# Where the experts' results are stored from: SyncE's queue or ScalarE's

## The reference, cut to what matters

```
buf = jnp.zeros((E, C, D), dtype=x.dtype).at[chosen_e, pos_c].add(x_flat * kept[:, None].astype(x.dtype))
h = jax.nn.gelu(jnp.einsum('ecd,edf->ecf', buf, w1) + b1[:, None, :], approximate=False)
eo = jnp.einsum('ecf,efd->ecd', h, w2) + b2[:, None, :]
y = eo[chosen_e, pos_c] * (chosen_p * kept.astype(x.dtype))[:, None]
```

## Time and profile before

| | us |
|---|---|
| Median of three runs (3335.19 to 3336.39) | 3335.85 |
| The profiled execution | 3335.44 |
| Its span, first to last instruction | 3333.7 |

### The profile page before, as it was taken

The page is one execution under the profiler, slowest core; times in us unless marked ns, Lnnn a source line. Parts: engine busy times, 40 slices in busy tenths (PEclk is TensorE's granted clock), DMA queues, the critical chain, the costliest instruction groups (busy, mean ns, idle before and its releaser), DMA issues. The chain is left out here.

```text
span 3333.7 us, 98254 instructions
## 1 busy us (share of the span) xinstructions
PE 3019.8 (91%) x27585; PEld 2232.3 (67%) x27741; DVE 2417.5 (73%) x8136; ACT 2248.4 (67%) x8822; POOL 1391.3 (42%) x2572
## 2 busy tenths in 40 slices
PE   7999998999999999999999996777996999977777
PEld 4555555788888888888888874555664666654444
DVE  6888887677777777777777773114665899978886
ACT  6888887666666666666666663224774999975554
POOL 5777775122222222222222210004663777757775
PEclk9999999999999999999999998998997999989999
DMA  5000000100000000000000001221000000000000
GB/s 150 0 0 0 0 0 11 70 5 6 5 4 4 5 4 5 5 5 5 5 5 4 12 3 46 68 77 30 17 17 6 7 6 7 6 4 7 13 19 13
DMA packets 80374, 54.49 MB, mean 16 GB/s; under 512 B 24801, under 2 KB 74413, under 8 KB 80160
## 3 DMA queue, kind: packets, MB, share of 16 engines
q1 hardware_dynamic: 76192, 45.26, 4.8%
q0 software_dynamic: 4096, 8.16, 0.8%
HBM read 32.66 MB, written 20.97 MB: 16 GB/s over the span
## 5 line engine op out<-in xcount | busy, mean ns | idle before, releaser
L1100 DVE COPY b_prT<-b_tr 128x512 f32<-128x512 f32 x512 | 352.0, 687 | 237.8 <-PE b_tr L991 233.4
L1359 ACT ACTIVATE b_pr<-b_sc,b_low 128x205 f32<-128x205 f32 x1024 | 431.1, 431 | 33.9 <-DVE b_low L1076 33.9
L473 ACT ACTIVATE a_pr<-a_sc,a_low 128x128 f32<-128x128 f32 x1024 | 360.8, 387 | 11.7 <-DVE a_low L376 6.9
L1091 DVE TENSOR_SCALAR b_pn<-b_pr,b_rec 128x205 f32<-128x205 f32 x1024 | 298.5, 334 | 55.0 <-DVE b_rec L1085 0.3
L1417 POOL TENSOR_TENSOR b_ln_var<-b_ln_mean_var,all_eps 128x1 f32<-128x1 f32 x64 | 12.1, 189 | 757.8 <-DVE b_ln_mean_var L152 757.8
L991 PE MATMUL b_tr<-all_ident,b_pn 128*128 128x128 f32 x2048 | 323.0, 280 | 5.3 <-DVE b_prT L1100 3.1
L2149 ACT ACTIVATE f_pr<-f_sc,f_low 128x77 f32<-128x77 f32 x1024 | 316.0, 333 | 13.8 <-DVE f_low L2057 13.7
L512 POOL TENSOR_TENSOR a_pn<-a_pr,a_rec 128x512 f32<-128x512 f32 x256 | 261.2, 1042 | 123.1 <-DVE a_rec L384 106.8
L991 PEld LDWEIGHTS b_tr<-all_ident,b_pn 128*128 128x128 f32 x2048 | 227.0, 141 | 87.0 <-issue 79.2
L1076 DVE TENSOR_REDUCE b_low<-b_sc 128x4 f32<-128x820 f32 x256 | 256.2, 1001 | 9.3 <-PE b_sc L979 9.3
L979 PE MATMUL b_sc<-b_kT,b_q 64*128 64x205 f32 x2048 | 247.2, 359 | 0.0
(11 more groups left out here) (307 smaller groups left out, 8170.5 us busy)
## 6 DMA issues: line engine op xcount, KB each, us to landing
scratch_x<-b_zeros SPq DMA_DIRECT2D x12, 512.0 KB, 5.2
b_vm<-scratch_x SPq DMA_DIRECT2D x24, 256.0 KB, 3.0
scratch_y<-b_vt SPq DMA_DIRECT2D x24, 256.0 KB, 2.4
all_X<-in_x SPq DMA_DIRECT2D x8, 512.0 KB, 6.9
e_w<-in_e_w SPq DMA_DIRECT2D x16, 256.0 KB, 3.0
out_x<-all_X SPq DMA_DIRECT2D x8, 512.0 KB
w_mask<-in_mask SPq DMA_DIRECT2D x1, 2464.0 KB, 10.3
b_cT<-in_ctxT SPq DMA_DIRECT2D x32, 77.0 KB, 2.0
```

The costliest lines, as they stand in the source:

```text
L473: op = act.activation(pr[:, g, u], sc[:, g, 128 * u:128 * u + 128], ACT.Exp, bias=low[:, g, u:u + 1], scale=-1.0, accum_out=sums[:, g, u:u ...
L1091: op = dve.tensor_scalar(pn[:, j % 2, g, 0:KN], pr[:, j % 2, g, 0:KN], rec[:, j % 2, g:g + 1], None, ALU.mult)
L1100: dve.tensor_copy(prT[:, j % 2, i].rearrange("p h t q -> p (h t q)"), tr[:]).then_inc(prT_made, 1)
L1359: op = act.activation(pr[:, j % 2, g, 0:KN], sc[:, j % 2, h, KN * i:KN * i + KN], ACT.Exp, bias=low[:, j % 2, g:g + 1], scale=-1.0, accum_ ...
```

## The change

The store of a group's results leaves SP's stream and goes to ScalarE's. It stands there behind the four Gelu activations of group n and stores group n-2, ahead of what ScalarE does for the FP4 weights in that step. Its wait for the addition, the buffers and the semaphore that it signals are the same. The last two stores follow the last pair on ScalarE. SP keeps the loads of rows and weights and, at the end, the wait for all stores.

```diff
@@ sync(sp), body @@
                     sp.dma_start(xr[:, k % 2], x_rows[n]).then_inc(x_loaded[k % 2], 16)
-                    if not (isinstance(j, int) and j == 0 and k < 2):
-                        store(n - 2, k % 2)
-
-        def store(n, ring):
-            sp.wait_ge(y_done, n + 1)
-            sp.dma_start(y_rows[n], yr[:, ring]).then_inc(stored[ring], 16)
 
         over_pairs(sp, body)
-        store(N * E // 2 - 2, 0)
-        store(N * E // 2 - 1, 1)
         for s in stored:
             sp.wait_ge(s, 16 * (E // 2) * G)
@@ scalar(act) @@
+
+        def store(n, ring):
+            act.wait_ge(y_done, n + 1)
+            act.dma_start(y_rows[n], yr[:, ring]).then_inc(stored[ring], 16)
 
         def body(j):
...
                     act.activation(hT[k % 2][:, f], ph[:, f // 2, f % 2], ACT.Gelu, bias=b1[:, r, f:f + 1])\
                         .then_inc(h_done, 1)
+                if not (isinstance(j, int) and j == 0 and k < 2):
+                    store(n - 2, k % 2)
                 if isinstance(j, int) and j == 0 and 0 <= k - FIRST - 2 < 3:
                     copy_weight(k - FIRST - 2)
                 if isinstance(j, int) and j == 0 and 0 <= k - FIRST < 3:
                     fp4_magic(act, fp4, consts, k - FIRST, (k - FIRST) % 2)
 
         over_pairs(act, body)
+        store(N * E // 2 - 2, 0)
+        store(N * E // 2 - 1, 1)
```

## The result

| | Median, us | Range | Runs |
|---|---|---|---|
| Before | 3335.52 | 3335.06 to 3336.39 | 4 |
| After | 3281.57 | 3280.56 to 3282.26 | 4 |

The ratio after to before is 0.9838, 95% interval 0.9821 to 0.9855. The profiled execution after took 3280.56 us, with a span of 3278.8.

The account below looks back on a forecast made before the run. TensorE bounds the experts but waits for loads queued on SP behind stores awaiting fresh additions. 39.1 + 10.1 + 2 - 2.55 = 48.7 us, taken as 49, gave 3287 us; range 3283 to 3293.

Parts of the forecast that it names:

- step 3: Pipeline overlap in the experts: each of 19 removed waits hides another 0.06 to 0.16 us; 2 us gained.
- step 5: Weight copies behind the stores on ScalarE make TensorE's transposes of groups 4, 5 and 6 wait: 2.55 us added.
- Step 1: TensorE's 19 waits for gathered token rows in the experts, after the first, all go: 39.1 us gained.
- Step 2: Slow clock in transposes and down matmuls behind the long load waits goes: 10.1 us gained.
- The second count: Check by start times of TensorE's groups up to transpose 23, with steps of 7.55 us: 49.1 us gained.
- Step 4: A store issue on ScalarE behind the Gelus costs 0.4 us, hidden in 21 of 24 groups.
- the clock was given back: Answers the rival that stretches of the experts stay at 1.2 GHz: 10 us less gain, 3297 us; 6%.
- ScalarE did not become the bound: Answers the rival that stores hold ScalarE and delay the next Gelus: 3349 us at 7 us per store; 2%.
- Only the issue time is saved: Rival: something else holds the loads back; 0.4 us in each of 22 steps, 9 us gained, 3327 us; 3%.

Follow-up runs that it names:

- e2: Changed kernel with only the stores ahead of a new expert's weights on ScalarE, the others back on SP: 3299.3 us (0.9883 of before).
- e3: Changed kernel with the stores ahead of a new expert's weights back on SP, the others on ScalarE: 3328.3 us (0.9972 of before).
- e4: Changed kernel with each store split into four DMAs of 64 KB, issued in a row by ScalarE: 3287.3 us (0.9849 of before).
- e5: Changed kernel with the three FP4 weight copies moved ahead of the Gelus of their group: 3278.7 us (0.9822 of before).
- e1: Kernel before with all stores kept on SP, each one slot later, behind the next load: 3282.7 us (0.9834 of before).
- e6: e1 with the three FP4 weight copies moved ahead of the Gelus of their group: 3278.9 us (0.9819 of before).
- e7: e3 with one more SP wait: an expert's second load is issued only when its first has landed: 3325.2 us (0.9957 of before).
- cb2: Kernel before, no edit, profiled a third time, on the same chip as its second profile: 3336.5 us.

## Why the prediction was wrong

The mechanism was right; the sizes of two terms were not. The sum of 48.7 us was 3.4 short of what the stretch gave, 52.1: the pipeline overlap (step 3) was taken at 2 us and measured 4.2, and the added waits (step 5) at 2.55 us and measured 1.4. The other 2 us up to the medians' 54.0 come with a profile of before whose stretch was short, and the range had no room for either.

- **Step 1, the load waits:** all 19 went. The slack at a new expert was smaller than worked out: the 11 us left out the addition's own time. For group 12 the addition ends at 2114.04, the first weight DMA goes out at 2114.28 and the load at 2116.45, and the transposes start at 2123.96, so 9.7 and 7.5 us. The loads took longer, 3.5 us in the median and 5.5 at most, which stayed hidden. Right in what it gives, and worth 39.1 in the profile used, 40.3 in the other two.
- **Step 2, the slow clock:** right in kind; e2 and e3 separate it from the short waits. Its size is not a constant: 10.1 us in the first profile, 12.2 and 11.6 in the two others (89.8 and 15.8 + 0.45 taken off). With step 1 that makes the stretch 3 us longer than in the profile from which I subtracted; by the mean of the three profiles it falls by 54.1 us, as the medians do. The total of the first profile did not give this away, since its time behind the experts was 2.4 us long: 52.1 + 2.4 + 0.4 ahead of the stretch are the 54.9 us between the two profiled executions.
- **Step 3, the pipeline overlap:** the term that was mis-sized in the sum itself. I took 2 us for 19 waits. A wait costs its row and 0.22 us: before, the step from group 16 to 17 took 2199.44 - 2190.85 = 8.59 us with a wait of 0.92, and the same step without takes 7.45, a difference of 1.14. The first 0.16 is the modelled end of up; the other 0.06 is in the transposes, 0.66 behind a wait and 0.60 without. 19 times 0.22 is 4.2. My bounds, 1.1 to 3.0, left out the second part. The lower one was a misreading too: the 3.54 us are those of the up of 3.70 (2041.11 to 2044.65), which also gives 0.16, so the rows had 3.0 to offer where I took the middle. The second count, 3.0 us short, had a fault of the same kind in another place: its step of 7.55 came from the one unwaited step in the trace, and that began with an up of 3.70 us behind a wait for DVE, 0.1 longer than the others. 17 steps make 1.8 us of the 3.0; step 5 makes the rest.
- **Step 4, the issue on ScalarE:** 0.38 us, as priced, and hidden.
- **Step 5, the three places without cover:** wrong by the 0.4 us each. I had the issue after the last Gelu; it runs beside it, and only what is longer than the Gelu would show (e4). The new wait at group 6 came, 1.25 us instead of 1.75. With the overlap, group 6 gives back 9.22 - 7.45 - 0.33 = 1.4 us (0.33 for the three weight transposes, by e5's steps of 7.78 against 7.45), where I took 2.55 for all three. The upper bound of 1.07 us for an issue was not the dearest in the trace either: the scatter's on L1451 take up to 1.23 us; it did not matter.

With the measured sizes the sum is 39.1 + 10.1 + 4.2 - 1.4 = 52.0, and the stretch fell by 52.1.

The rivals: the clock was given back in full. ScalarE did not become the bound. "Only the issue time is saved" is refuted twice, since e1 saves no issue on SP and gains the same, and e6, with the issues on SP, is as fast as e5. The sentence of the Trainium skill (DMA: Bandwidth & Descriptors, Issuing engines are not separate DMA queues) is thereby borne out for what it speaks of: another issuing engine gave nothing here, 3282.7 against 3283.1 us. The gain here was another one: a wait that stood in a queue ahead of a load that did not need it.

## What to carry to other kernels

When an engine waits for a load, look at what its queue waited for ahead of the issue; a store that waits for a fresh result may stand behind the next loads instead of on another engine, and here it gained the same. Price a removed wait by the difference between a step with it and one without, not by its row, and add the slow clock behind the long ones. Where such clock is part of the sum, one profile is one draw: take two or three, or widen the range by what it could have been.

## What the runs showed of the hardware

- A DMA issue in ScalarE's queue runs beside an activation that is already under way: 0.38 us inside a Gelu of 0.69; four take 1.79 us, and the next activation starts only behind them (e4).
- Loads of 256 KB landed after 3.0 us (median) while each stood behind a store in SP's queue, before and in e1, and after 3.5 in the kernel after. A second load directly behind is one cause: the median is 4.1 us in e3 and 3.2 in e7, which holds that load back. Whether the stores of the other queue are another was not tried. Stores stayed at 2.3 to 2.5.
- Of the 35 waits of 3.4 to 5.1 us in the three profiles of before, e3 and e7, 33 were followed by matmuls at the 1.2 GHz level and two were not (group 18 in the first profile of before, 3.56 us, and group 9 in cb2, 3.75 us, each with a down of 3.74). Waits of up to 1.8 us never were, and of the three of 2.5 us in e4 one was. How much was lost behind the seven waits differs from profile to profile: 10.1, 12.2 and 11.6 us in before. The spread of the times does not measure it: e3, with seven long waits, spread over 8 us in seven runs, but e6, without any from group 2 on, over 5.5 in five.
